# Gate weights' low parts before the expert gathers, and the first expert product before the second turn, in a four-layer graph and expert network

## The reference, cut to what matters

```python
logits = xf @ gate_w + gate_b                    # 8 experts
top2_vals, top2_idx = jax.lax.top_k(softmax(logits), 2)      # layer 1
h = gelu(xf @ W1[e] + b1[e]); y = h @ W2[e] + b2[e]          # 256 -> 512 -> 256
out = sum over the two experts of weight * y
```

## Time and profile before

| | us |
|---|---|
| median of 3 runs (lowest, highest) | 2132.79 (2129.72, 2132.90) |
| the profiled execution, its own time | 2132.07 |
| its span, first to last instruction | 2130.0 |

### The profile page before, as it was taken

One profiled execution on the slowest core, in us unless ns is written; L12 is line 12 of the kernel. 1 busy time (PEld: TensorE's weight loads), 2 busy tenths in 40 slices (PEclk: granted clock), 3 DMA queues, 4 the chain that ended last, 5 costly groups with the idle time before them and its releaser, 6 DMA issues.

```text
span 2130.0 us, 41957 instructions
## 1 busy us (share of the span) xinstructions
PE 1864.8 (88%) x15580; PEld 1262.1 (59%) x15580; DVE 1517.3 (71%) x3193; ACT 1129.8 (53%) x2228; POOL 454.2 (21%) x531
## 2 busy tenths in 40 slices
PE   6999486999999999865995899949967999999998
PEld 3788343678888888764673588837754222222344
DVE  6877655667777758875666677555666788989786
ACT  7565366634434334534784556536656435455466
POOL 0000474201100103314672111127720000002010
PEclk9999688999999999986997999959988999999999
DMA  7999355668888979965677666162232333322100
GB/s 215 341 348 356 127 147 163 215 241 297 318 320 300 332 271 357 390 237 201 198 246 258 166 179 198 40 224 88 90 110 84 115 96 114 97 79 79 56 18 36
DMA packets 236570, 412.55 MB, mean 194 GB/s; under 512 B 20303, under 2 KB 188879, under 8 KB 217616
## 3 DMA queue, kind: packets, MB, share of 16 engines
q1 hardware_dynamic: 213108, 361.52, 50.0%
q0 software_dynamic: 13760, 39.68, 6.2%
q10 hardware_dynamic: 9504, 8.65, 1.2%
HBM read 316.02 MB, written 93.78 MB: 192 GB/s over the span
## 4 chain that ended last, share of the span: by engine, by line
PE 65%; DVE 18%; ACT 6%; issue 4%; DMA 4%; POOL 2%; SPq 0%; ACTq 0%; DVEq 0%; POOLq 0%
PE ps L2972 9%; PE ps L1129 9%; PE ps L1131 8%; PE ps L1130 8%; PE ps L2978 5%; PE ps L294 4%; PE ps L296 4%; PE ps L295 4%; PE ps L2604 3%; PE ps L2606 2%; DVE BIG L3172 2%; DVE BIG L1700 1%; DVE bst L518 1%; DMA BIG<-in_adj 1%; PE ps L2577 1%
## 5 line engine op out<-in xcount | busy, mean ns | idle before, releaser
L1129 PE MATMUL ps<-R,BIG 128*128 128x256 f16 (+1 forms) x1764 | 482.3, 273 | 3.0 <-ACT BIG L1595 2.4
L1131 PE MATMUL ps<-R,BIG 128*128 128x256 f16 (+1 forms) x1764 | 479.7, 272 | 0.0
L1130 PE MATMUL ps<-R,BIG 128*128 128x256 f16 x1764 | 479.3, 272 | 0.0
L2972 PE MATMUL ps<-BIG 128*64 128x452 f32 x1056 | 230.9, 558 | 22.3 <-DVE BIG L3172 20.0
L3172 DVE SCALAR_TENSOR_TENSOR BIG<-BIG 128x904 f32<-128x904 f32 x176 | 198.9, 1193 | 34.5 <-PE ps L2978 23.9
L1129 PEld LDWEIGHTS ps<-R,BIG 128*128 128x128 f16 x1764 | 170.5, 97 | 29.5 <-issue 3.0
L1130 PEld LDWEIGHTS ps<-R,BIG 128*128 128x128 f16 x1764 | 172.5, 98 | 20.4
L1131 PEld LDWEIGHTS ps<-R,BIG 128*128 128x128 f16 x1764 | 170.6, 97 | 23.2
L2972 PEld LDWEIGHTS ps<-BIG 128*64 128x64 f32 x1056 | 64.4, 136 | 181.2 <-issue 137.1
L3052 ACT ACTIVATE BIG<-X,BIG 128x64 f32<-128x64 f32 x264 | 70.2, 337 | 170.0 <-PE ps L2978 170.0
L294 PE MATMUL ps<-X,BIG 128*128 128x256 f16 (+1 forms) x568 | 138.8, 256 | 5.0 <-ACT X L2631 3.7
(11 more groups left out here) (475 smaller groups left out, 4392.7 us busy)
## 6 DMA issues: line engine op xcount, KB each, us to landing
BIG<-adj_split SPq DMA_DIRECT2D x63, 1376.0 KB, 6.3
BIG<-in_adjT SPq DMA_DIRECT2D x29, 1408.0 KB, 10.6
BIG<-in_adj SPq DMA_DIRECT2D x22, 1408.0 KB, 10.6
BIG<-in_adjT SPq DMA_DIRECT2D x66, 452.0 KB, 3.3
adj_split<-BIG SPq DMA_DIRECT2D x21, 1376.0 KB
XX<-in_f SPq DMA_DIRECT2D x70, 256.0 KB, 7.8
experts_split<-XX SPq DMA_DIRECT2D x64, 256.0 KB
BIG<-experts_split SPq DMA_DIRECT2D x16, 1024.0 KB, 13.3
```

Source lines behind the costliest of these rows:

```text
L1129: pe.matmul(out[:, 0:n], pr[:, 0, k, :], h[:, k, 0:n], start=start, stop=False)
L1130: pe.matmul(out[:, 0:D], pr[:, 0, k, :], l[:, k, 0:D], start=False, stop=False)
L1131: return pe.matmul(out[:, 0:n], pr[:, 1, k, :], h[:, k, 0:n], start=False, stop=stop)
L2972: pe.matmul(ps[rs, 2 * (h // 2) + c, 0:CW], self.G[:, u, h * HF:(h + 1) * HF], self.PT[:, u, h, cs], start=start, stop=stop)
```

## The change

The changed kernel differs in four places. In layer 1 the loads of the expert weights wait for four semaphores in place of eight. GpSimd makes the low parts of the next layer's gate weights in `Route(1)` and `Route(2)`, in front of the gathers of `Experts`, and no longer at q == 3. SyncE starts the loads of later weights in layer 1 after the second turn, and no longer after the end of the route. TensorE reads the expert words first, then turns group 0, makes its first product, and only then turns group 1; ScalarE's order is changed to match.

```diff
@@ class P1, __init__
                 self.freed = [self.st.end(n) for n in ("used", "rl", "cb", "w0", "w1", "w2", "w3", "d4")]
+                self.places = [self.st.end(n) for n in ("used", "rl", "cb", "d4")]
@@ class Route
             def sp(self, sp):
-                for s, v in self.prod.freed:
+                for s, v in self.prod.freed if self.i != 1 else self.prod.places:
                     sp.wait_ge(s, v)
...
             def pool(self, pool):
                 F[self.i].pool(pool)
+                if self.i:
+                    W[self.i + 1].pool(pool)
@@ class Experts, sp
-                after(sp, self.route)
+                s.wait(sp, "t3", 2)
@@ class Experts, pool
-                    if q == 3:
-                        W[self.i + 1].pool(pool)
@@ class Experts, pe
-                turn(0)
-                turn(1)
                 for z, n in self.route.done:
                     pe.wait_ge(z, n)
                 words += expert_words(pe, E1)
+                turn(0)
                 hidden(0)
+                turn(1)
@@ class Experts, act
                 turned(0)
+                hidden(0)
                 turned(1)
-                hidden(0)
```

## The result

The changed kernel takes 2136.29 us (median of 12 runs, 2132.01 to 2138.29). The kernel before, run beside it, takes 2131.92 us (12 runs, 2129.72 to 2137.16). The ratio is 1.0019 with an interval of 1.0011 to 1.0027. By the ratio it is 4.1 us slower, 2.3 to 5.8; the two medians differ by 4.4. Forecast was +1.4 us, 2134.2. The slowdown is real, since the whole interval lies above 1, but it is of the size of the 0.2% that the prediction took as its bound for "no change". The profiled execution took 2135.54 us. Lines have moved by one to three against the kernel before (L2577 is L2578, L2544 is L2547).

The account below looks back on a forecast made before the run. Bound mostly by TensorE work in the chain of waits, with small holes at stage borders. Layer 1 +0.4 and layer 2 +1.0 made +1.4 us (0 to 4.3), so 2134.2 us; range 2128 to 2140.5.

Parts of the forecast that it names:

- the sign of the sum: Layers 1 and 2 together: slower by 1.4 us, within 0 to 4.3.
- Part 1, places: Layer 1's expert weight loads: `rl` still holds SyncE; dropped waits gain 0 to 0.3 us, taken as 0.
- Part 2, layer 1: Low parts ahead of layer 1's gathers: first gather 6.1 to 7.0 us later, 3.2 us of TensorE waits gone.
- the first rival: Layer 1's GpSimd: configuration change not hidden, 7.9 us more before the gathers, 2142.1 us; chance 0.12.
- Part 2, layer 2: Low parts beside DVE's last index work: DVE held 0.6 us (0 to 2), turn 0 at 1420.6.
- Part 3: First product ahead of second turn: product 1 starts 7.7 to 8.2 us after product 0, giving back 2.6 us.
- the third rival: Engines hold each other longest in layer 2, clock's rise falls between products 0 and 1: 2138.5 us; chance 0.08.
- Part 4: Layer 1's loads of later weights wait for the second turn: 12 us left for a load, cost nothing.
- Second rival: Layer 1's places come free early, all loads 7.3 us earlier: 2128.4 to 2129.0 us; chance 0.10.

Follow-up runs that it names:

- places_undone: The changed kernel with layer 1's expert weight loads waiting for all eight semaphores again; 2137.36 us against 2131.44 for the kernel before, ratio 1.0023.
- config_touch: The kernel before plus one unused one-column subtraction on GpSimd behind the all-reduce; 2127.66 us against 2131.68, ratio 0.9982.
- split: The changed kernel with the second turn between the halves of product 0, its copy between the halves of group 0's activations; 2129.35 us against 2131.58 for the kernel before.
- changed_words: The changed kernel with words first but both turns ahead of product 0; 2128.11 us against 2131.58 for the kernel before, ratio 0.9991.
- low_layer1: The changed kernel with layer 2's low parts back at q == 3; 2134.75 us against 2131.68 for the kernel before, ratio 1.0014.
- order_only: The kernel before with only the new order of TensorE and ScalarE; 2133.91 us against 2132.19, ratio 1.0009.
- low_only: The kernel before with only the gate weights' low parts moved into the routes, ahead of the gathers; 2135.73 us against 2132.19, ratio 1.0015.
- order_undone: The changed kernel with the old order of TensorE and ScalarE (both turns, words, product 0); 2133.26 us against 2131.68 for the kernel before, ratio 1.0012.

## Why the prediction was right or wrong

The time was inside the range and the sign of the sum was right, but +1.4 became +4.1, near the upper end of the 0 to 4.3 that the sum allowed. The mechanism was right where it says that gathers come late, that product 1 waits for its copy and that the configuration change hides. The size is partly luck: in layer 1 a fall of the clock that the sum left out was half made up by a start that came earlier than forecast. Point by point, all of it moved to the zero of the kernel before:

- **Part 1, places.** Right: `rl` holds the loads. The gain was 0.28 us at the loads, the upper end of the range that I gave. I had not seen that the high parts can inherit it: here they start 0.9 us earlier than before, counted from the zeros, of which `places_undone` puts about 0.5 down to the dropped waits.
- **Part 2, layer 1.** Right in kind. Low parts at 977.0, gather at 980.7 and turn 0 at 985.0, each about 0.8 earlier than forecast (977.8, 981.6, 985.8). Product 0 at 987.3, forecast 988.3. The holes of 3.2 us are gone and the configuration change is hidden, so the first rival fell: its MODIFY_POOL_CONFIG is at 945.5 and nothing stands before the low parts. `config_touch` shows what was hidden, 9.2 us. The Trainium skill's sentence on it (GPSIMD Engine Reference, "Instruction dispatch") gives approximately 6 us; the runs show 7.4 to 10.4.
- **Part 2, layer 2: the step that was sized wrong.** I took 0.6 us for DVE held by GpSimd, within 0 to 2; it was 1.55. I also left out that the words come from the same engine behind the index: their reading began 8.5 instead of 6.9 us after zero. And it took TensorE 2.6 us, not the 2.1 that I had worked out from ScalarE's row. With the words now ahead of the turn it is they, not the gather, that let turn 0 start: 8.5 + 2.6 = 11.1 from zero. That is 1422.1 where I took 1420.6, just outside 1420.0 to 1422.0. This, less 0.1 elsewhere, is the 1.4 us by which layer 2 missed. The Trainium skill's rule of an exclusive lock, held for a whole instruction (SBUF — State Buffer, "SBUF: two separate sides"), gave up to 3.6 us. The trace agrees with such a hold: three DVE steps each ended with one of the low parts. But the delay in front of `idxg` was 1.55 and not 3.6 us, because the first low part held nothing (only the two steps that read `ps` ran beside it and the next) and the second held a step for 0.3 us alone. The other half of my sentence, that both engines slow each other, was wrong here: the low parts kept their 3.55 us.
- **Part 3.** Right: product 1 7.94 and 7.49 us behind product 0, forecast 7.7 to 8.2 (layer 2 a little under it). `split` and `changed_words` show that this is what the order gives back.
- **Part 3, the clock: left out of the sum.** That the clock would be low in product 1 stood in the third rival, put into layer 2 with a chance of 0.08, as a rise that comes late. What happened was another thing, in layer 1: the clock rose in product 0 and fell again, and that cost 1.7 us. With 0.3 us less won from the holes, and product 1 0.8 us earlier than forecast (+2.8, not +3.6), that is layer 1's miss: +1.5 for +0.4. It is not certain in an execution: in layer 1 it is seen in three of four profiles with the hole there, and not in `low_layer1`; in layer 2 in none of the four, and in two of those (`order_only`, `low_layer1`) it had not risen before the hole.
- **Part 4.** "Cost nothing" was right for the side that I looked at, the later use: ScalarE waited 1.5 us in all for such blocks, TensorE not at all from 997.38 to 1127.7. I did not ask what the loads collide with. Alone, with the four places, they are worth -2.8 us. In the changed kernel the second gather is no longer waited for in front of product 0, and there the gain is only that the late first gather is not slowed: 4.3 us from gather to turn, against 5.5 in `low_only`.
- **Second rival** (places free 7 us early): fell, the loads still start at `rl`.

What stays open. The sums of single profiles of `order_undone` and `low_layer1` (-0.1 and -0.2 us over both layers) do not agree with their medians (+2.6, +3.0); for the other kernels the two differ by up to 2.2 us. So the miss is explained in kind, and its parts only as well as one profile of each kernel can tell. How often the clock falls back in the hole was not measured, and with it how much of the 4.1 is due to it. The dropped waits were not tried alone in the kernel before.

## What to carry to other kernels

A step that is moved to where its engine idles has to be read from the other engines too: here the low parts stood on idle GpSimd, but in front of the gathers and beside the index work on which the whole stage waits. When a one-time cost hangs on the first instruction of a kind, bring it forward with a tiny instruction of that kind, and leave the work where it was. And when work is put ahead of a wait, follow the second item through both engines: the first product came earlier only for the second to wait for its copy.

## What the runs showed of the hardware

- On GpSimd the configuration change belongs to the first TENSOR_TENSOR behind the all-reduce; neither copies nor all the gathers and scatters up to q == 3 brought it. It takes 7.4 to 10.4 us from then (7.9, 7.4, 9.2 and 10.4 in four kernels), and costs nothing if they pass idle. Other kinds of operation were not tried.
- Reading a word into a register took 0.53 us on ScalarE and 0.66 on TensorE, four in a row. TensorE's own waits do not name it: the row says "issue", or blames a ScalarE copy.
- DVE operations of 50 columns beside GpSimd's low parts took 0.52 to 0.86 us instead of 0.19 to 0.25, each ending within 0.06 us of the end of a low part, and the low parts lost nothing. Two operations that read `ps` beside them lost nothing either.
- TensorE's clock went up in product 0 and, after 16 transposes and a hole of 1.96 us, back to 1.2 GHz; with the same work in the same order another execution stayed at 2.4 GHz.
- An indirect gather of two tiles slowed from 4.3 to 5.5 us when 256 KB loads began beside it (`order_undone`, `low_only`).
